# A graph network kernel: the second pass takes 15 sorted blocks and 44 gathered groups where it took 14 and 48

## The reference

```python
h = relu(layernorm(x))
h = relu(mean_over_edges(h[src] @ W1.T + b1, dst))     # pass 1
x = x + mean_over_edges(h[src] @ W2.T + b2, dst)       # pass 2
h = relu(layernorm(x))
m = relu(concat(h[src], emb[edge_type]) @ msg_W.T + msg_b)
agg = segment_sum(m, dst) / max(deg, 1)                # pass 3
out = layernorm(h + agg @ upd_W.T + upd_b) * ln_g + ln_b
return x + out
```

## Time and profile before

| | us |
|---|---|
| median of three runs | 1861.92 |
| lowest, highest | 1856.38, 1866.67 |
| profiled execution | 1866.55 |
| span in it, first to last instruction | 1864.8 |
| TensorE, VectorE, GpSimd, ScalarE busy | 1618.7, 1365.2, 1292.3, 982.2 |

### The profile page before, as it was taken

The page is one execution under the profiler, slowest core; times in us unless marked ns, Lnnn a source line. Parts: engine busy times, 40 slices in busy tenths (PEclk is TensorE's granted clock), DMA queues, the critical chain, the costliest instruction groups (busy, mean ns, idle before and its releaser), DMA issues.

```text
span 1864.8 us, 42446 instructions
## 1 busy us (share of the span) xinstructions
PE 1618.7 (87%) x15761; PEld 1377.4 (74%) x15761; DVE 1365.2 (73%) x3742; ACT 982.2 (53%) x1951; POOL 1292.3 (69%) x1318
## 2 busy tenths in 40 slices
PE   0189989989999967999999899849999999999996
PEld 0067777877777755777777777648998988899895
DVE  6767878878887463566666666467788888898886
ACT  3656666757766545777777777532222222222322
POOL 2087777777777617777777777657777776677772
PEclk9999999999999978999999999959999999999998
DMA  3334434344444336445555555636566666666662
GB/s 107 121 97 115 119 107 112 107 116 123 119 114 111 104 115 182 129 130 142 161 142 144 150 136 150 168 118 171 172 198 174 171 189 170 174 175 182 176 171 76
DMA packets 160332, 262.92 MB, mean 141 GB/s; under 512 B 30949, under 2 KB 126775, under 8 KB 160119
## 3 DMA queue, kind: packets, MB, share of 16 engines
q1 hardware_dynamic: 109944, 157.28, 28.6%
q0 software_dynamic: 50176, 102.84, 21.8%
HBM read 236.89 MB, written 23.11 MB: 139 GB/s over the span
## 4 chain that ended last, share of the span: by engine, by line
POOL 28%; PE 16%; issue 12%; DVE 4%; DMA 3%; ACT 1%; DVEq 0%; POOLq 0%
POOL rows L829 28%; PE banks L1172 16%; DMA rows<-table,src_all 3%; DVE region_a L2051 1%; DVE region_a L2257 0%; DVE htab L2262 0%; DVE agg L1989 0%; POOL region_b L842 0%; DVE rows L2077 0%; DVE x_or_cnt L1775 0%; DVE src_hot L2038 0%; DVE region_b L1976 0%; DVE stats L1800 0%; DVEq L1983 0%; DVE region_b L2036 0%
## 5 line engine op out<-in xcount | busy, mean ns | idle before, releaser
L829 POOL DMA_INDIRECT rows<-table,src_all x1184 | 1236.5, 1044 | 479.1 <-issue 440.1
L1172 PE MATMUL banks<-region_a 128*128 128x256 bf16 (+2 forms) x6168 | 1018.6, 291 | 2.3 <-DVE region_a L1590 2.3
L1135 ACT ACTIVATE region_a<-banks 128x384 bf16<-128x384 f32 x1456 | 671.7, 500 | 326.8 <-PE banks L1172 326.5
L1172 PEld LDWEIGHTS banks<-region_a 128*128 128x128 bf16 (+2 forms) x6168 | 691.8, 118 | 154.7 <-issue 4.7
L1172 PE MATMUL banks<-htab,src_hot 128*128 128x128 bf16 (+2 forms) x3484 | 631.6, 267 | 65.5 <-DVE src_hot L2038 32.9
L1172 PEld LDWEIGHTS banks<-htab,src_hot 128*128 128x128 bf16 x3484 | 288.7, 99 | 123.3 <-ACT region_a L1135 45.5
L1172 PE MATMUL banks<-hot,rows 128*128 128x128 bf16 (+1 forms) x3136 | 254.9, 239 | 63.1 <-DMA rows<-table,src_all 56.7
L1172 PEld LDWEIGHTS banks<-hot,rows 128*128 128x128 bf16 (+1 forms) x3136 | 240.8, 125 | 76.5 <-issue 54.3
L2038 DVE TENSOR_SCALAR src_hot<-src_in,part_no 128x768 bf16<-128x768 bf16 (+1 forms) x328 | 147.8, 452 | 130.6 <-PE banks L1172 115.4
L2051 DVE TENSOR_SCALAR region_a<-columns,slot_dst 128x256 f32<-128x256 f32 x676 | 210.6, 378 | 0.0
L1142 ACT ACTIVATE region_a<-banks 128x896 f32<-128x896 f32 (+1 forms) x104 | 88.9, 855 | 192.2 <-PE banks L1172 186.6
(11 more groups left out here) (214 smaller groups left out, 1080.0 us busy)
## 6 DMA issues: line engine op xcount, KB each, us to landing
src_in<-src_tab SPq DMA_DIRECT2D x164, 224.0 KB, 3.4
src_in<-src_tab SPq DMA_DIRECT2D x164, 192.0 KB
region_b<-in_etype SPq DMA_DIRECT2D x52, 512.0 KB, 6.0
rows<-table,src_all POOLq DMA_INDIRECT x1184
region_b<-type_tab SPq DMA_DIRECT2D x52, 224.0 KB, 5.3
region_b<-type_tab SPq DMA_DIRECT2D x52, 192.0 KB
table<-htab SPq DMA_DIRECT2D x14, 384.0 KB, 3.4
table<-htab SPq DMA_DIRECT2D x14, 288.0 KB, 3.6
```

Of the source, the lines that this page charges most:

```text
L829: nc.gpsimd.indirect_dma_start(out=to[:, c, :], out_offset=None, in_=tab[layer], in_offset=bass.IndirectOffsetOnAxis(ap=cols[:, c:c + 1], ...
L1135: nc.scalar.activation(picked[u % 2][:, j, :], pick_ps[t % 4], ACT.Copy)\
L1172: return nc.tensor.matmul(to, left, right, start=start, stop=stop)
```

## The change

`NB[1]` goes from 14 to 15, so `NG[1]` goes from 48 to 44. The fifteenth block (number 14, edges of groups 56 to 59) is sorted in pass 1 like the others; pass 1 itself still has 14 blocks, so `digits_of` and the counts are not run for it. Tables are sized by `SORTED`, and `EXTRA` blocks (two, formerly one) get their destinations relative to the block's first node. The chain on `far` handles two blocks in place of one. ScalarE waits for the last stored codes ahead of `make_rows`, since the room of `code_T` is used again there. SyncE waits for a block's codes ahead of loading block 14 in pass 2. Two small arrays move into `hot` to save room.

```diff
-    NB = (B + 1, B + 1, B)
-    OFF = (0, B + 1, 2 * (B + 1))
+    NB = (B + 1, B + 2, B)
+    OFF = (0, NB[0], NB[0] + NB[1])
+    SORTED = max(NB)
+    EXTRA = SORTED - B
...
-    BLOCK_COLS = (B + 1) * BLOCK_C
+    BLOCK_COLS = SORTED * BLOCK_C
...
-        type_f = sb("type_f", [P, 3, F])
-        type_p = sb("type_p", [P, K3, F], bf16)
...
+        type_f = hot[0][:, C // 2:C // 2 + 3, :]
...
+                        elif layer == 1 and b >= NB[0] and u == 0:
+                            sp.wait_ge(code_T_stored, 32 * (b + 1))
...
-                        if layer == 0 and u == U - 1 and b < B:
+                        if layer == 0 and u == U - 1 and b + 1 < SORTED:
                             store_codes(b + 1, b + 2)
...
                 act.wait_ge(rinv_ready, 1)
+                act.wait_ge(code_T_stored, 32 * SORTED)
...
-                        if layer == 0 and u == 2 and b + 2 <= B:
+                        if layer == 0 and u == 2 and b + 2 < SORTED:
                             sort_before(b + 3)
-                        if layer == 0 and u == 3 and b < B:
+                        if layer == 0 and u == 3 and b + 1 < SORTED:
                             sort_table(b + 2)
...
                             elif u == 3:
-                                if b + 2 <= B:
+                                if b + 2 < SORTED:
                                     sort_first(b + 3)
                                 make_spread(b)
-                                if b < B:
+                                if b + 1 < NB[0]:
                                     digits_of(b + 1)
...
-                    own, beyond = mask[:, 0:BC], spare[:, 0:BC]
+                    own, beyond = mask[:, 0:EXTRA * BC], spare[:, 0:EXTRA * BC]
```

More of the change, by code:

```diff
@@ L776, in _ @@
                 sp.wait_ge(out_stored[k], 16 * len(range(k, NV, 3)))
-            sp.wait_ge(code_T_stored, 32 * (B + 1))
+            sp.wait_ge(code_T_stored, 32 * SORTED)
         @block.gpsimd
@@ L1124, in step @@
                     for u in range(U):
-                        if layer == 0 and u == 3 and b + 2 <= B:
+                        if layer == 0 and u == 3 and b + 2 < SORTED:
                             tile_rows(b + 3)
@@ L1357, in step @@
                             block_count(b)
-                        if layer == 0 and u == 5 and b < B:
+                        if layer == 0 and u == 5 and b + 1 < SORTED:
                             sort_turn(b + 2)
@@ L2161, in _ @@
                             lambda: V.reduce_max(far_max[:, 0:1], far[:, :], axis=AX.X))
-                    last = slice(B * BC, (B + 1) * BC)
-                    own, beyond = mask[:, 0:BC], spare[:, 0:BC]
-                    chained(lambda: V.tensor_copy(far_group[:, :], far[:, last]),
+                    own, beyond = mask[:, 0:EXTRA * BC], spare[:, 0:EXTRA * BC]
+                    now = (NB[0] - B) * BC
+                    chained(lambda: V.tensor_copy(far_group[:, :], far[:, extra]),
                             lambda: V.tensor_single_scalar(own, rel_last[:, :], 0.0, op=ALU.is_lt),
@@ L2168, in _ @@
                                                            op0=ALU.is_gt, op1=ALU.max),
-                            lambda: V.scalar_tensor_tensor(out=far_block[:, :], in0=rank1[:, last], scalar=float(2 * P),
+                            lambda: V.scalar_tensor_tensor(out=far_block[:, :], in0=rank1[:, extra], scalar=float(2 * P),
                                                            in1=far_block[:, :], op0=ALU.is_gt, op1=ALU.max),
-                            lambda: V.tensor_tensor(own, tile_no[:, last, 0], first_tile[:, FIRST_GROUP:FIRST_GROUP + 1]
-                                                    .broadcast_to([P, BC]), ALU.subtract),
+                            lambda: V.tensor_tensor(by_block(own), by_block(tile_no[:, extra, 0]), first_of_block(first_tile), ALU.subtract),
                             lambda: V.tensor_single_scalar(beyond, own, 0.0, op=ALU.is_lt),
@@ L2175, in _ @@
                                                            op0=ALU.is_gt, op1=ALU.max),
-                            lambda: V.scalar_tensor_tensor(out=beyond, in0=rank1[:, last], scalar=float(P), in1=beyond,
+                            lambda: V.scalar_tensor_tensor(out=beyond, in0=rank1[:, extra], scalar=float(P), in1=beyond,
                                                            op0=ALU.is_gt, op1=ALU.mult),
                             lambda: V.tensor_tensor(far_block[:, :], far_block[:, :], beyond, ALU.max),
-                            lambda: V.scalar_tensor_tensor(out=own, in0=dst_all[:, last], scalar=1.0, in1=far_block[:, :],
+                            lambda: V.scalar_tensor_tensor(out=own, in0=dst_all[:, extra], scalar=1.0, in1=far_block[:, :],
                                                            op0=ALU.add, op1=ALU.mult),
                             lambda: V.tensor_single_scalar(far_block[:, :], own, -1.0, op=ALU.add),
-                            lambda: V.tensor_copy(far[:, last], far_block[:, :]),
+                            lambda: V.tensor_copy(far[:, B * BC:B * BC + now], far_block[:, 0:now]),
                             lambda: V.reduce_max(far_max[:, 1:2], far_block[:, :], axis=AX.X),
@@ L2205, in _ @@
                     ADDS = 3 * WINDOWS + 1
-                    if layer == 2:
-                        V.tensor_copy(far[:, B * BC:(B + 1) * BC], far_group[:, :]).then_inc(far_swapped, 1)
+                    if layer == 1:
+                        V.tensor_copy(far[:, NB[0] * BC:NB[1] * BC], far_block[:, now:(NB[1] - B) * BC]).then_inc(far_swapped, 1)
                         dve.wait_ge(far_swapped, 1)
+                    elif layer == 2:
+                        V.tensor_copy(far[:, extra], far_group[:, :]).then_inc(far_swapped, 1)
+                        dve.wait_ge(far_swapped, 2)
                     def fb_group(g, first):
```

55 lines of the change are left out of this document (30 added, 25 removed).

## The result

| | before | after |
|---|---|---|
| median, measured side by side | 1858.49 | 1844.15 |
| lowest, highest of 6 runs each | 1854.97, 1866.67 | 1843.35, 1848.1 |
| ratio to before, 95% interval | | 0.992, 0.9899 to 0.9941 |
| profiled execution, its span | 1866.55, 1864.8 | 1844.23, 1842.5 |

Measured again at the end on another chip, the changed kernel had 0.9929 (0.991 to 0.9949). The change makes the kernel 13 to 15 us faster. I had forecast 8.3 us and a range of 1846 to 1868; 1844.15 lies under it, so the forecast missed. About 3.4 us of the distance to my 1853.6 is the baseline, since before came out at 1858.49 and not at 1861.92; the other 6 us are mine. Three executions took far longer than all others (9341.42 us of the kernel before, 3396.21 of "before, from unit 4", 3868.33 of "both"): the ratios leave them out, the medians have them in.

The account below looks back on a forecast made before the run. GpSimd's gathers were taken to bound the second pass, with TensorE the bound after the change. Second pass -9.8 and first pass +1.5 summed to -8.3 us, 1853.6 from the median of 1861.9, range 1846 to 1868.

Parts of the forecast that it names:

- TensorE's 32.0 us a block: Second pass after the change: TensorE needs 26.7 + 3.9 + 1.4 = 32.0 us a block, GpSimd 30.5.
- block less four sums: Second pass, TensorE: the fifteenth block adds 26.7 us and four group sums fewer save 5.4.
- waits for rows: Second pass, TensorE: waits for gathered rows fall from 39.3 to 12.2 us, saving 27.1.
- slow clock: Second pass: of some 6 us lost to the lower clock behind waits for rows, 5 are saved.
- of the other 27.2 I keep 3, for late landings: Second pass: of the 27.2 us of waits beyond the three largest, 3 us stay.
- gaps of 2, 2: Second pass: consecutive two-unit gaps left 14.5 us between freeing and using a slot; the new list leaves at least 17.8.
- I let 1.9 of the 2.7 disappear in waits that would be there anyway, and keep 0.8: First pass, blocks 12 and 13: of TensorE's 2.7 us of added sort work, existing gather waits hide 1.9, costing 0.8.
- the waits hide all and also the slow clock behind them: First pass, lower bound for TensorE's added sort work: -2 us.
- the waits stay (1873): Rival, second pass: waits come from two slots and landing time, 15 us stay; +11 in all, 1873 us; chance 0.1.
- the gathers stretch with VectorE's load (1871): Rival, second pass: a busier VectorE lengthens a gather group to 11.5 us; +9 in all, 1871 us; chance 0.07.
- the sort isn't hidden (first pass +6): Rival, first pass: TensorE's 2.7 us and late masks cost +6, not +1.5; all -4, 1858 us; chance 0.2.
- The fallback: Rival: an edge of the fifteenth block falls outside its window and a fallback costing milliseconds runs; chance 0.01.

Follow-up runs that it names:

- before, from unit 4: Kernel before (14 blocks, 48 groups) with its second-pass sums placed from unit 4 on instead of unit 1; 1863.74 us, ratio 0.9995.
- both: Changed kernel with fifteen blocks in the first pass too and second-pass sums placed from unit 4 on; 1845.96 us, ratio to before 0.9907.
- Before with seven gathers of eight: Kernel before with the eighth gather of each second-pass group left out, TensorE's work unchanged; 1830.07 us, ratio 0.983.
- the change with seven: Changed kernel with the eighth gather of each second-pass group left out, TensorE's work unchanged; 1841.14 us, ratio to before 0.9895.
- the pair with sums from unit 4: Second-pass sums placed from unit 4 instead of unit 1, in the changed kernel (1840.05 us, ratio 0.9881) and in the kernel before (1863.74 us, 0.9995).
- The sort alone: Changed kernel with the fifteenth block sorted but not used, second pass at 14 blocks and 48 groups; 1857.46 us, ratio to before 0.9988.
- before again: Kernel before with no edit, run for a second profile; 1859.93 us, ratio 1.0002.
- after again: Changed kernel with no edit, run again on a third chip, also called the change again; 1849.83 us, ratio to before 0.9929.
- The bunched places: Changed kernel with its 44 second-pass sums placed at gaps of 2, 2, 4 and 3 units; 1850.67 us, ratio to before 0.9943.
- the repeated table alone: Kernel before with block 12's 32 table matmuls issued a second time in the first pass's last block; 1860.44 us, ratio 0.9978.

## Why the prediction was right and wrong

**The bound: right.** Before, GpSimd sets the second pass and the change hands it to TensorE. Before with seven gathers of eight (-37 us in the pass) and the change with seven (-0.2) show it, and so does the pair with sums from unit 4. TensorE's 32.0 us a block came out at 31.94, and that includes ScalarE's waits (2.2 us in these 13 blocks), which I had put on top; so its own need is some 0.2 us a block less than I said.

**The sum of the second pass: right sign, too small.** -9.8 was said, -18.1 measured in the two profiled executions. Four executions with before's second pass gave 507.1 to 511.2, four with the change's (one of them with seven gathers of eight) 491.0 to 493.9, so -16.8 between their means. The terms, from the two profiled executions:

| term | said | measured |
|---|---|---|
| block less four sums | +21.3 | +19.2 (449.4 to 468.6) |
| waits for rows | -27.1 | -31.5 (39.3 to 7.8) |
| slow clock | -5 | -5.7 (11.1 to 5.4) |
| ScalarE | +1 | -1.8 (5.3 to 3.5) |
| VectorE's mask and sum | 0 | +2.1 |

The slow clock is the sum, over stretches of 5 us from the first gather to the last block sum, of 5 us times (1 - clock). The first row is TensorE's busy time in the pass (460.5 and 474.0 us) less that; the runs with seven gathers of eight gave 18.8 for it. The measured terms add up to -17.7, against -18.1 for the whole. The step that failed most in this pass is "of the other 27.2 I keep 3, for late landings": nothing was left of them, and the first three groups kept 7.8 us where I had 9.2. GpSimd pauses for 29.6 us over the pass, so it is ahead, and behind the first block a landing that is late is late for nobody. The block was 2.1 us cheaper than I had it, less its four sums. ScalarE's waits went the other way than I said; why, no run tells.

The times say less than the traces. The sort alone had 0.9988 and the change 0.992, so the 15 and 44 are worth 12.6 us with some 5 of uncertainty (11 by the repeat's 0.9929). The profiled executions of before and of the sort alone were 8 and 7 us above their medians; the two closest to theirs, before again and after again, have passes that differ by 13.3. So the second pass gave 11 to 17 us, and not clearly the 18.1 of one pair. Of the 6 us that I was off by the medians, the larger part may be the first pass's (-2.2 for +1.5).

My argument on gaps of 2, 2 was wrong in its reason. The bunched places show that such gaps cost nothing behind the start. The waits left all belong to the first block: one to the first group, where GpSimd has no lead, the other, as the rows have it, to the load of `x`. I had priced the third group's wait by its place alone (1.7, it was 1.90) and had not named that load, though the earlier trace rows show its full DMA engines; and I had no term for the mask that is late behind it.

**The first pass: wrong sign.** The step was "I let 1.9 of the 2.7 disappear in waits that would be there anyway, and keep 0.8"; its bound said -2 "the waits hide all and also the slow clock behind them", and that is what happened. In the prediction's own terms, the clock behind the second wait of block 13 was left low and priced at nothing in the sum. With the table ahead of it, the group that was waited for 2.41 us isn't waited for at all, its matmuls take 1.50 and not 2.74 us, and the buckets behind it don't run at half clock; block 12 gives back 1.4 to 2. The sort alone measured -2.2 us (0.9988, interval up to 1.0002), the repeated table alone -4.1. I had seen the half clock in the second pass and priced it there, and had the row of 2.74 us in my own list for the first; I didn't take it as the likely case.

**Rivals.** That the waits stay (1873) is out: two waits are left. (Its sum, 26.7 - 5.4 - 15 + 3, had a 3 that I gave no source for and that no run shows.) That the gathers stretch with VectorE's load (1871) is out: VectorE's share rose from 0.60 to 312.19 / 493.00 = 0.63 and a gather went from 996 to 986 ns. The prediction read the gathers' lengths by how busy VectorE is; single rows of before say that it is by what VectorE does (last section). By the rule of the Trainium skill (SBUF — State Buffer, Who interferes with whom) more masks of the tensor_scalar kind could have cost GpSimd time; 13 blocks at a steady 31.94 us with GpSimd pausing don't show that. That the sort isn't hidden (first pass +6) is out, by the sort alone. The fallback didn't run.

**The marks I had set.** Waits to about 12: 7.8. Blocks 32 to 33 us apart: 31.94. The last gather 15 us and more ahead of the last sum: it ended at 1170.5, 14.0 ahead. The pass ends near 1198: 1184.5, of which 4.6 is its earlier start. The last block of pass one at most 3 us longer: with what follows it, it was 4 us shorter. The test chain not later than 650: it began at 642.58.

## What to carry to other kernels

When two engines feed a pass in turns, price a shift of work by each one's need per block, and then expect nearly all waits of the faster one to vanish once the other has a lead, except those at the start, where no lead exists yet, and those behind another transfer that fills the DMA engines: look for it by the DMA share of the stretch in which the wait stands. Move the first uses later only when the feeder is no longer the bound. Look for a wait of 2 us and more on a busy TensorE with matmuls of doubled length behind it: independent work put ahead of such a wait can save more than it costs (here 4 us for 1.6), and that belongs in the forecast and not only in its bounds.

## What the runs showed of the hardware

- In the last block of the first pass, waits of 2.41 to 2.60 us on a TensorE that was otherwise busy came with half clock for about 7 us (24 matmuls in 2.74 us for 1.50), and one of 2.12 us with less of it (2.07). Waits of 1.3 to 1.5 us in the same block left the clock at 1.00. The length of the wait alone doesn't decide, though: in the trace of before, the group behind a wait of 3.17 us at 377.37 took 1.51 us and the clock fell only behind it, and one of 2.23 us at 1063.29 left the clock at 1.00; in the change again 1.87 us at 142.88 was enough for 2.74. 32 matmuls of 1.72 us ahead of the wait, which went with it, saved 4.1 us (1.3 to 6.7) of the whole.
- A load of `x` that took 17.4 to 20.0 us from its issue went with a share of the DMA engines of 0.93 to 1.07 and 248 to 318 GB/s for some 15 us. In the twelve executions in which TensorE waited for a group in that time, its rows came 5.8 to 7.0 us behind its last gather; those of the first group of the pass, where it was waited for, 1.8 to 2.2 us, and those of groups waited for later in the trace of before 1.9 to 4.3 us.
- Gathers were longer beside some kinds of VectorE's work and not beside others. In the traces of before and after, gathers of the first pass that ran beside nothing but a scan of 442 columns took 1.46 and 1.56 us on average (16 and 21 of them), and beside a tensor_tensor mask of 1792 columns 1.45 and 1.32 us (11 and 10); in the second pass, beside tensor_scalar masks of 256 columns, 0.97 and 0.96 us (75 and 74), and beside nothing 0.95. Over whole passes it is 986 to 1001 ns in each second one, with 14 or 15 blocks, and 1107 to 1129 in each first.
